# Mamba and mixture-of-experts layer: dt*x*B of two groups of states made together, TensorE's other products in four bundles between, and the small operations of the other engines moved after them

## Time and profile before

| what | value |
| --- | --- |
| runs, us | 1363.46, 1358.88, 1363.42; median 1363.42 |
| profiled execution | span 1386.3 us; no other time of its own is recorded |
| busy share of the span | PE 93%, PEld 58%, DVE 79%, ACT 66%, POOL 63% |
| chain that ended last, by engine | PE 61%, DVE 11%, issue 6%, DMA 1% |
| TensorE clock granted | 0.986 of full on average |
| DMA | 304.82 MB, mean 220 GB/s; queue of SyncE 63.3% of the 16 engines |
| stretches | stage 1 to 271 us; recurrence to 1080 us, DMA share about 0.9 and 270 to 280 GB/s; stage 3 after |

### The profile page before, as it was taken

One profiled execution on the slowest core, in us unless ns is written; L12 is line 12 of the kernel. 1 busy time (PEld: TensorE's weight loads), 2 busy tenths in 40 slices (PEclk: granted clock), 3 DMA queues, 4 the chain that ended last, 5 costly groups with the idle time before them and its releaser, 6 DMA issues.

```text
span 1386.3 us, 53429 instructions
## 1 busy us (share of the span) xinstructions
PE 1291.9 (93%) x21591; PEld 808.3 (58%) x21591; DVE 1095.9 (79%) x1257; ACT 910.5 (66%) x1914; POOL 878.1 (63%) x522
## 2 busy tenths in 40 slices
PE   4999989699999999999999999999999899999998
PEld 3767767445555545555555555545554577787876
DVE  4798989878988889888888898888898655646554
ACT  3756567478788788887887888777777343434343
POOL 2455448268888988988889889889898421303030
PEclk9999999789999999999999999999999999999999
DMA  8153534859898998998989989989889761313130
GB/s 289 65 224 118 218 120 172 272 170 297 257 295 274 283 269 257 304 280 248 306 259 279 288 248 308 285 252 290 263 255 300 243 231 51 132 45 137 37 144 30
DMA packets 129710, 304.82 MB, mean 220 GB/s; under 512 B 18512, under 2 KB 20304, under 8 KB 127824
## 3 DMA queue, kind: packets, MB, share of 16 engines
q1 hardware_dynamic: 122048, 285.13, 63.3%
q0 software_dynamic: 7600, 18.91, 6.0%
HBM read 213.91 MB, written 56.77 MB: 195 GB/s over the span
## 4 chain that ended last, share of the span: by engine, by line
PE 61%; DVE 11%; issue 6%; DVEq 1%; DMA 1%; ACT 0%; POOL 0%; ACTq 0%; POOLq 0%
PE p_dBx L1313 18%; PE p_y L1322 9%; DVE state L1002 8%; PE p_dBx L1372 7%; PE p_g L1299 6%; PE p_g L1282 6%; PE p_dt L1262 2%; PE p_y L1383 2%; PE p_g L1383 2%; PE p_u L1383 2%; PE p_dt L1383 2%; PE p_u L1268 2%; DVE out_operand_parts L1037 2%; PE p_u L1289 1%; PE p_u L1282 1%
## 5 line engine op out<-in xcount | busy, mean ns | idle before, releaser
L1002 DVE TENSOR_TENSOR_SCAN state<-dA,state_carry,p_dBx 128x512 f32<-128x512 f32 x512 | 626.9, 1266 | 104.3 <-PE p_dBx L1313 96.8
L937 POOL TENSOR_TENSOR h_times_C<-state,C_bcast 128x1024 f32<-128x1024 f32 x128 | 307.1, 2400 | 87.4 <-DVE state L1002 86.6
L1313 PE MATMUL p_dBx<-B_diagonals,step_rows 64*32 64x128 f32 x16384 | 327.9, 275 | 30.0 <-issue 20.4
L1313 PEld LDWEIGHTS p_dBx<-B_diagonals,step_rows 64*32 64x32 f32 x16384 | 242.3, 106 | 178.8 <-issue 176.8
L937 POOL TENSOR_TENSOR C_bcast<-state,C_bcast 128x1024 f32<-128x1024 f32 x128 | 319.9, 2787 | 18.1 <-DVE state L1002 18.1
L1152 ACT ACTIVATE dA<-dt_blocks_odd,A_par 128x512 f32<-128x512 f32 x256 | 169.7, 710 | 14.8 <-DMA dt_blocks_odd<-step_rows 14.8
L1152 ACT ACTIVATE dA<-dt_blocks_even,A_par 128x512 f32<-128x512 f32 x256 | 169.7, 710 | 4.2 <-DMA dt_blocks_even<-step_rows 4.2
L276 POOL TENSOR_TENSOR w_in_parts_lo<-C_bcast,w_in_parts_hi 128x512 fp32r<-128x512 f32 x64 | 89.8, 1406 | 113.0 <-ACT w_in_parts_hi L485 112.8
L952 POOL TENSOR_TENSOR step_rows<-step_rows 128x512 f32<-128x512 f32 x16 | 21.9, 1401 | 182.3 <-DMA step_rows<-moe 182.3
L364 DVE SCALAR_TENSOR_TENSOR conv_out<-conv_in,conv_w,conv_out 128x512 f32<-128x512 f32 x96 | 100.4, 1055 | 10.3 <-ACT conv_out L499 8.0
L1299 PE MATMUL p_g<-w_down_pair,step_rows 128*64 128x512 f32 (+1 forms) x396 | 92.3, 601 | 0.0
(11 more groups left out here) (184 smaller groups left out, 2111.1 us busy)
## 6 DMA issues: line engine op xcount, KB each, us to landing
w_gate_pair<-in_w_gate SPq DMA_DIRECT2D x32, 1408.0 KB
w_up_pair<-in_w_up SPq DMA_DIRECT2D x32, 1408.0 KB, 8.0
w_down_pair<-in_w_down SPq DMA_DIRECT2D x66, 512.0 KB
dt_blocks_odd<-step_rows SPq DMA_DIRECT2D x256, 64.0 KB
dt_blocks_even<-step_rows SPq DMA_DIRECT2D x240, 64.0 KB
w_down_pair<-in_w_down SPq DMA_DIRECT2D x33, 384.0 KB
g_d<-y_gated SPq DMA_DIRECT2D x33, 256.0 KB, 4.8
sz_d<-silu_gate SPq DMA_DIRECT2D x32, 256.0 KB, 2.0
```

Of the source, the lines that this page charges most:

```text
L937: pool.tensor_tensor(hc[m][:, b, :, :], hb[:, q, :, :], Cb[:, NM * cp + GS * m:NM * cp + GS * m + GS, :], ALU.mult).then_inc(s_hc, 1)
L1002: ins = dve.tensor_tensor_scan(hb[:, g % NBUF, s, :], dA[:, g % NBUF, s, :], pB[:, g % 2, :].rearrange("p (t s) -> p s t", s=GS)[:, s, :], ...
L1313: ins = pe.matmul(out[DB * p:DB * p + DB, half, j, :, :], dtxT[k, j * P + DB * b:j * P + DB * b + DB], diag[k, ND * cp + 2 * j + p // 2, a ...
```

## The change

The placement constants get new values, among them two new names. TensorE's order becomes dBx(0), dBx(1), dt, transposes of h, gate, dBx(2), dBx(3), sum, up, dBx(4), dBx(5), transposes of dt*x, down, dBx(6), dBx(7), transposes of the next pair's tokens, sum. The first pair's tokens are transposed ahead of the loop. The small operations of VectorE and ScalarE move to other groups. SyncE issues w_down ahead of x.

```diff
-DT_AT, GATE_AT, HH_AT = 1, 3, 5
-WEIGHT_AT, SOFTPLUS_AT, SILU_AT, DT_COPY_AT, DIAG_AT = 2, 3, 4, 5, 6
+DT_AT, GATE_AT, HG_AT, HH_AT = 2, 3, 3, 5
+WEIGHT_AT, SOFTPLUS_AT, HT_AT, SILU_AT, DT_COPY_AT, DIAG_AT = 2, 4, 4, 5, 6, 3
...
                     tile_in.load_up(sp, i + 1)
...
+                sp.wait_ge(s_yps, i + 2)
+                load_wd(i + 1)
                 sp.wait_ge(s_sum, 2 * i + 3)
                 if i + 2 < STEPS:
                     tile_in.load_xa(sp, i + 2)
...
-                sp.wait_ge(s_yps, i + 2)
-                load_wd(i + 1)
...
-                            if g == HH_AT:
+                            if g == HG_AT:
                                 dve.wait_ge(s_sg, i + 1)
                                 dve.wait_ge(s_hTps, i + 1)
                                 dve.tensor_tensor(hh[:, :], sg[:, :], pG[:, 0:I], ALU.mult).then_inc(s_hg, 1)
-                            if g == HH_AT + 1:
+                            if g == HH_AT:
...
+                            if g == SILU_AT + 1:
+                                act.wait_ge(s_se, 2 * i + 1)
+                                act.activation(sg[:, :], sg[:, :], ACT.Ln, bias=1.0).then_inc(s_se, 1)
+                                act.wait_ge(s_se, 2 * i + 2)
+                                act.activation(sg[:, :], sg[:, :], ACT.Exp, scale=-1.0).then_inc(s_sg, 1)
                             act.wait_ge(s_scan, NG * i + (g + 1))
...
-                            if g == SILU_AT + 1:
+                            if g == HT_AT:
                                 take_hT(i)
-                                act.wait_ge(s_se, 2 * i + 1)
...
+            pe.wait_ge(s_hh, 1)
+            tokens_T(0)
...
                     dBx(i, cp, 0)
-                    pe.wait_ge(s_hh, i + 1)
-                    tokens_T(i)
+                    dBx(i, cp, 1)
                     pe.wait_ge(s_dxT[1], i + 1)
                     dt_proj(i + 1)
-                    dBx(i, cp, 1)
                     pe.wait_ge(s_xT, i + 1)
+                    transpose_h(i)
                     pe.wait_ge(s_yo, i + 1)
                     pe.wait_ge(s_wg, 16 * i + 16)
                     gate_or_up(pG, wg, range(KH), s_gps)
                     dBx(i, cp, 2)
+                    dBx(i, cp, 3)
                     sum_states(i, 1, 1)
-                    transpose_h(i)
-                    dBx(i, cp, 3)
                     pe.wait_ge(s_hT, i + 1)
                     pe.wait_ge(s_wu, 16 * i + 16)
-                    gate_or_up(pU, wu, range(KH // 2), s_ups)
+                    gate_or_up(pU, wu, range(KH), s_ups)
                     dBx(i, cp, 4)
-                    gate_or_up(pU, wu, range(KH // 2, KH), s_ups)
+                    dBx(i, cp, 5)
                     dtx_T(i + 1)
-                    dBx(i, cp, 5)
+                    pe.wait_ge(s_hg, i + 1)
+                    down(i)
                     dBx(i, cp, 6)
+                    dBx(i, cp, 7)
+                    pe.wait_ge(s_hh, i + 2)
+                    tokens_T(i + 1)
                     pe.wait_ge(s_xD, i + 1)
                     sum_states(i, 0, 0)
-                    dBx(i, cp, 7)
-                    pe.wait_ge(s_hg, i + 1)
-                    down(i)
```

More of the change, by code:

```diff
@@ L1168, in steps @@
                                 act.activation(sg[:, :], pG[:, 0:I], ACT.Exp, scale=-1.0).then_inc(s_se, 1)
-                            if g == SILU_AT + 1:
+                            if g == HT_AT:
                                 take_hT(i)
-                                act.wait_ge(s_se, 2 * i + 1)
-                                act.activation(sg[:, :], sg[:, :], ACT.Ln, bias=1.0).then_inc(s_se, 1)
-                                act.wait_ge(s_se, 2 * i + 2)
-                                act.activation(sg[:, :], sg[:, :], ACT.Exp, scale=-1.0).then_inc(s_sg, 1)
                             if g == DIAG_AT and c == NCH - 1 and u == 1:
```

## The result

The changed kernel takes 1457.84 us (median of 4 runs, 1451.39 to 1464.02) against 1362.85 (4 runs): ratio 1.068, 95% interval 1.064 to 1.072. The forecast was 1400 in a range of 1340 to 1420. The direction and the path that sets the step came as forecast. The size did not, and the time lies outside the range. The profiled execution is the run of 1451.39 us, with a span of 1449.6.

What follows compares the result with a forecast made beforehand. TensorE was taken to set the 24.9 us step; after the change the path through SyncE's queue and x would set 26.2. 31 x (26.2 - 24.9) = +40, less 3 absorbed, +37 on 1363.4: 1400 us, range 1340 to 1420.

Steps and rivals of the forecast that it cites:

- TensorE's share: Sign of the forecast: TensorE's busy share should fall to about 91%.
- The scans' round trip of 24.0: VectorE and TensorE alternating in the new order: 17.4 us of scans plus 6.6 of TensorE, against 24.9 now.
- Rival 2: Faster: x lands early, pauses covered, the scans' round trip of 24.0 to 24.3 sets the step; 1336 to 1345 us; chance 0.24.
- One sign: VectorE's scans should wait for dt*x's group, not for dBx.
- the sum's base: Present step of 24.9 us, and the runs' median of 1363.4, 23 us below the profiled span, difference carried over.
- the path's length: Closed path through SyncE's queue: dt*x and copy 1.4, issues 11.2, landing of x 13.5, hop 0.1; 26.2 us.
- 3 us be absorbed: At chunk changes, part of the 8 us absorbed since TensorE no longer bounds; 3 us by estimate.
- The 37 us forecast: Total over the recurrence: 31 x (26.2 - 24.9) = +40 us, less 3 absorbed at chunk changes.
- one sentence: ScalarE: softplus and diagonals (together 4.7 us) move ahead of the copy of dt, which comes at about 12 us.
- Rival 1: TensorE's pauses follow GpSimd's gather and scatter onto dBx(2) and dBx(7): step 24.8 to 25.3, 1360 to 1376 us; chance 0.18.
- The pair of dBx: Two dBx together on TensorE: 2.32 us against 2 x 1.08 apart; no gain, up to 0.1 us lost per pair.
- four tails saved: If mode changes cost the 0.2 us tail behind each dBx, 0.8 us of TensorE's step saved; the sum took zero.

Runs made afterwards that it cites:

- both paths and both pauses were out of the way: Changed kernel with x issued ahead of w_down, copy of dt at group 5, diagonals at 6, GpSimd's gather and scatter moved: 1382.6 us, ratio 1.016.
- the execution of 1375: The kernel before, unchanged, profiled a second time: 1375.1 us beside a median of 1364.3, mean step 24.56 us.
- x first: Changed kernel with only SyncE's queue put back, x for dt*x issued ahead of the three w_down loads: 1420.5 us, ratio 1.040.
- the kernel without it: Changed kernel, w_down still ahead of x, with copy of dt at group 5 and diagonals at 6: 1452.1 us, ratio 1.045.
- x first, copy at 5, diagonals at 6: Changed kernel with x issued ahead of w_down, copy of dt at group 5 and ScalarE's diagonals at group 6: 1412.4 us, ratio 1.018.
- Before, copy at 4: Kernel before with the copy of dt at group 4 in place of 5: 1393.5 us, ratio 1.004.
- its second set: The changed kernel run again, unchanged: 1467.1 us beside 1366.1 for the kernel before, ratio 1.076.

## Why the prediction was wrong

**Right.** The edit that decides is the order of SyncE's queue, and the path consists of the terms that were forecast: dt*x 0.7, hop and copy, 16 issues and w_up 11.2 in most steps, then x behind w_down. x lands 13.9 us behind w_up's issue (mean of 30 steps) where 13.5 stood. TensorE's share is 89% (91 forecast), and VectorE sits idle for x before dt*x in 30 of 31 periods. The scans' round trip of 24.0 was near: the shortest steps are 23.62 where both paths and both pauses were out of the way. Rival 2 needed x under 11.5 us in the changed kernel; the shortest of the 30 landings is 11.6. One sign did not come: the scans' idle time is still ended by dBx, 98.4 of 98.6 us.

**The step that failed is the sum's base.** The prediction set 26.2 against the 24.9 of the steps read in the profiled execution, and carried the 23 us between its span and the runs over to the result "as it is". But a path made of issues and landings does not shrink when TensorE's pauses do: the changed kernel's spans lie 2 us under its runs, and it takes 1458 and 1467 where before takes 1363 and 1366. A step of the kernel before at 1363 us is about 24.2, an estimate (24.56 in the execution of 1375, less 12 us over 31). Against the mean of 25.17 that is 31 x 0.97 = 30 us that the forecast counted as there already. TensorE's pauses, as read above, were what made the first profile long: 1.44 us a step in it at the third and eighth dBx, 0.41 in the second.

**The second term is the path's length.** Forecast 26.2, or 26.35 on average with the 5 us left at chunk changes; measured 27.09 over all 31: 31 x 0.74 = 23 us. Against the 26.2 of a step the 30 periods with the wait have 27.20, in three parts, as means of 30: from the first issue to w_up 11.5 and not 11.2 (the 16 issues take 11.4 to 12.2 us at the chunk changes, where I let 3 us be absorbed and nothing was); ScalarE holds the copy 0.4 us on average, 1.9 at most, which I took as zero; x 0.4 later. The 37 us forecast, with these 30 and 23, make 90 of the 95 us. The other 5 are not accounted for.

**What it did not see.** ScalarE was given one sentence, that softplus and diagonals move ahead of the copy of dt, and no price. They lengthen a second closed path, and with x first the mean step is 26.3. In the change as made it costs little beside the longer one: its share is the 0.4 us for which ScalarE holds the copy, and the kernel without it is at 27.11. But undoing the queue alone leaves 56 us where the whole change costs 95.

**Rival 1's mechanism is real and was put too low.** In the new order the pauses were 1.24 us at dBx(2) and (3) and 0.7 to 0.9 at dBx(7), a rigid 25.46 us a step once both closed paths were out of the way, 0.2 above its range.

**The pair of dBx.** The prediction took no gain from two dBx together. Undisturbed (x first, copy at 5, diagonals at 6):

```profile
564.47 2.09 PE L1314 MATMUL p_dBx<-B_diagonals,step_rows 64*32 64x128 f32 x128
566.50 1.12 PE L1263 MATMUL p_dt<-ts_tile,w_dt 32*128 32x512 f32 x2
```

2.03 us from its start to the next, against 1.09 for one alone (604.94 to 606.03 above): 0.15 us saved per pair. The order before has one pair already, dBx(5) and dBx(6), and the new one has four, so the change saves at most 0.45 us a step, in the changed kernel hidden behind the paths. The prediction counted four tails saved. The Trainium skill (TensorEngine Tiling (Array Packing), section Key Properties) says that a change of tiling mode drains the array. The trace is in line with it, 2.03 us together against 2 x 1.09 apart; the 0.8 us that the prediction worked out by it was too much, and its zero too little.

## What to carry to other kernels

- Look for every path that closes over one step, through in-order queues above all (a DMA queue, an engine's program), and sum each before a change: here the round trip of the scans (23.6 us), TensorE with its pauses (25.5), ScalarE and the spread (26.3 on average) and the queue of x (27.2) lay one behind the other, and each showed when the longer ones were out of the way. Work that stands in a wait for a transfer is free; the same work ahead of the instruction that starts the transfer lies on the path.
- In the one queue of SyncE, 1408 KB put ahead of the 256 KB of x moved its landing from 9.0 to 13.9 us behind the issue of w_up. Put first what closes the loop.
- When the bound changes, the difference between a profiled span and the runs must not be carried over: here it belonged to the old bound, TensorE with its pauses. Take a second profile before a sum in microseconds is built on the first.
- Compare a variant with the best version of its rival. A fix that helps both orders says nothing for one of them.

## What the runs showed of the hardware

- An indirect DMA of GpSimd stands beside a pause of TensorE in the small products of dBx, which ends 1.25 to 1.33 us behind the gather's start in all 30 steps (x first, copy at 5, diagonals at 6). The first profile of the kernel before had 1.44 us of pauses a step at its third and eighth dBx on average, the second 0.41. "Before, copy at 4", on a chip where the kernel before takes 1388 us, had 1.37, so the chips of this study seem to differ in these pauses. Why TensorE pauses is open.
- The load of x reports its landing in 16 parts, and dt*x goes with the last. In the changed kernel that one is 0.2 us behind the fifteenth in the median, but 3.6 once (w_up issued at 580.58, the fifteenth part 11.68 us later, the last 15.32) and 2.7 another time (635.63).
- TensorE's clock: in its first profile the kernel before ran the recurrence at the full level (2.4 GHz), 1.00. In the changed kernel the recurrence has a mean of 0.96, and stretches at the lower level (1.2 GHz) stand in it. The rows below show one of them and the stretch before it, in which TensorE sat idle while dt*x was late. Stretches in the order busy PE, PEld, DVE, ACT, POOL, then clock, DMA share, GB/s:

```profile
733.00:736.20 3.20, 1.54 (x80) 1.03 (x75) 3.20 (x4) 1.34 (x5) 0.25 (x1) 1.00 1.01 354
736.20:739.60 3.40, 3.40 (x70) 2.24 (x56) 3.40 (x5) 2.42 (x6) 2.52 (x3) 0.50 0.60 129
```

  TensorE worked 1.54 of 3.20 us, and then ran 3.4 us at 0.50. The mean clock of the changed kernel's runs is 0.951 to 0.965, of the kernel before beside its second set 0.979 to 0.984. What of the 95 us is the clock's was not separated.
